# One-core attention and expert-FFN kernel: orders of loads, maxima, probabilities and key projections changed in three attention batches and at the entry of the FFN

## The reference, cut to what matters

```python
def _bi_wkv(r, k, v, w, u, time_emb):     # r = x, k = v = side input
    decay = exp(-exp(w)) * (0.5 + 0.5 * tf)
    nf, df = scan(ekv, ek)                # forward:  a = a * decay + ekv_t
    nb, db = scan(ekv, ek, reverse=True)
    num = nf + nb - ekv + euk * vf
    den = df + db - ek + euk
    return sigmoid(r) * (num / maximum(den, 1e-08)) * (0.8 + 0.2 * tf)

def _L0_attn_ref(query, ...):
    q, k, v = split(query @ Wqkv.T + bqkv)              # 16 heads of 16
    attn = softmax(einsum('bhqd,bhkd->bhqk', q, k) * HD ** 0.5)
    return einsum('bhqk,bhkd->bhqd', attn, v) @ Wproj.T + bproj

def _L0_ffn_ref(x, ...):
    # w_dense: the best 6 of 64 experts, from the best 4 of 8 groups
    h = relu2(einsum('th,eih->tei', x, w1)) * w_dense[:, :, None]
    return einsum('tei,ehi->th', h, w2) + relu2(x @ shared_up.T) @ shared_down.T

x = x + attn(wkv(x, side, ...))
x = x + ffn(wkv2(x, side, ...))
```

## Time and profile before

| | us |
|---|---|
| median of 3 executions | 382.6 (382.35 to 384.66) |
| the profiled execution | 386.37 |
| its span, first to last instruction | 384.3 |
| around the span | 2.07 |
| busy: PE, DVE | 315.8, 319.8 |
| busy: ACT, POOL | 201.6, 129.1 |

### The profile page before, as it was taken

One profiled execution on the slowest core, in us unless ns is written; L12 is line 12 of the kernel. 1 busy time (PEld: TensorE's weight loads), 2 busy tenths in 40 slices (PEclk: granted clock), 3 DMA queues, 4 the chain that ended last, 5 costly groups with the idle time before them and its releaser, 6 DMA issues.

```text
span 384.3 us, 6121 instructions
## 1 busy us (share of the span) xinstructions
PE 315.8 (82%) x1626; PEld 248.8 (65%) x1626; DVE 319.8 (83%) x616; ACT 201.6 (52%) x381; POOL 129.1 (34%) x117
## 2 busy tenths in 40 slices
PE   0082288879678998877898999999999999999994
PEld 0062165658476876744676867788887888888882
DVE  6989999996699977759677999878888888888883
ACT  4113135553624475385447556566666666666651
POOL 2528435424331011032123334343333334343431
PEclk9996577896969999899899999999999999999999
DMA  5949908603550573125433555655556556665631
GB/s 188 160 80 124 191 7 106 112 8 63 96 61 1 103 99 66 69 65 169 140 111 114 168 163 172 191 183 195 196 180 197 185 193 186 195 185 184 194 132 55
DMA packets 36280, 50.79 MB, mean 132 GB/s; under 512 B 5474, under 2 KB 18082, under 8 KB 36258
## 3 DMA queue, kind: packets, MB, share of 16 engines
q1 hardware_dynamic: 36258, 50.52, 51.9%
HBM read 39.03 MB, written 1.33 MB: 105 GB/s over the span
## 4 chain that ended last, share of the span: by engine, by line
PE 52%; DVE 23%; issue 9%; ACT 5%; POOL 5%; DMA 3%; SPq 1%; DVEq 0%; ACTq 0%; POOLq 0%
PE ps L1357 7%; PE ps L1348 7%; PE ps L1346 7%; PE ps L1358 7%; PE ps L1347 7%; PE ps L1359 7%; DVE scan L778 5%; DVE mx L831 5%; PE ps L1184 3%; PE ps L1268 2%; DVE qk_lo L1106 2%; PE ps L1215 2%; ACT prob L520 1%; DVE q_st L986 1%; PE ps L1196 1%
## 5 line engine op out<-in xcount | busy, mean ns | idle before, releaser
L453 POOL TENSOR_TENSOR scan<-scan 128x512 f32<-128x512 f32 x68 | 73.0, 1074 | 130.6 <-ACT scan L583 130.6
L1106 DVE TENSOR_TENSOR qk_lo<-scan,qk_hi 128x512 fp32r<-128x512 f32 x68 | 70.2, 1032 | 26.9 <-ACT qk_hi L590 26.8
L583 ACT ACTIVATE scan<-ps 128x512 f32<-128x512 f32 x68 | 40.8, 600 | 48.3 <-PE ps L1348 48.2
L1357 PE MATMUL ps<-qk_hi,k_st 128*128 128x512 f32 x136 | 55.0, 404 | 3.4 <-DVE qk_lo L1106 3.4
L576 ACT ACTIVATE k_st<-clip 128x512 fp32r<-128x512 f32 x68 | 42.9, 632 | 27.1 <-PE ps L1359 25.4
L1346 PE MATMUL ps<-hid_hi,k_st 128*128 128x512 f32 x136 | 54.3, 399 | 0.8 <-DVE q_st L986 0.8
L1348 PE MATMUL ps<-hid_hi,q_st 128*128 128x512 f32 x136 | 54.2, 399 | 0.0
L1347 PE MATMUL ps<-hid_lo,k_st 128*128 128x512 f32 x136 | 53.9, 396 | 0.0
L1196 PE MATMUL ps<-k_st,q_st 96*128 96x256 f32 x128 | 31.6, 351 | 26.8 <-DVE mx L831 18.7
L1358 PE MATMUL ps<-qk_lo,k_st 128*128 128x512 f32 x136 | 53.4, 393 | 0.0
L1359 PE MATMUL ps<-qk_hi,q_st 128*128 128x512 f32 x136 | 53.3, 392 | 0.0
(11 more groups left out here) (122 smaller groups left out, 487.7 us busy)
## 6 DMA issues: line engine op xcount, KB each, us to landing
clip<-in_tiles SPq DMA_DIRECT2D x68, 256.0 KB, 3.0
ex<-gates SPq DMA_DIRECT2D x136, 128.0 KB, 2.9
q_st<-qk_hi SPq DMA_DIRECT2D x16, 128.0 KB, 3.8
q_st<-qk_lo SPq DMA_DIRECT2D x16, 128.0 KB, 4.7
k_st<-qk_hi SPq DMA_DIRECT2D x16, 128.0 KB, 5.1
k_st<-qk_lo SPq DMA_DIRECT2D x16, 128.0 KB, 5.2
f_sb<-in_fT SPq DMA_DIRECT2D x4, 256.0 KB, 8.8
x_sb<-in_xT SPq DMA_DIRECT2D x4, 256.0 KB, 8.9
```

Source lines behind the costliest of these rows:

```text
L453: g.tensor_tensor(sq[:, k], relu[:, k], relu[:, k], ALU.mult).then_inc(sq_ready, 1)
L1106: TT(act_lo[:, k], act[:, k], act_hi[:, k].bitcast(F32), ALU.subtract).then_inc(act_lo_ready, 1)
L1357: mm(acc, w_hi, act_hi[:, k], start=first, stop=False, skip_group_check=True)
```

## The change

No operation is added or removed. On five queues the order differs; the list `jobs` follows PE's order.

* SP, entry of the FFN: the weights of units 4 and 5 are loaded before the second store of gates, and not behind it.
* PE, batches 1 and 2: the next keys are projected in two pieces, ahead of `values(b - 1, 2)` and of `values(b - 1, 3)`, as batch 0 did already; before, in one piece behind `turn_out`. The gate product goes one head later. In batch 3 `turn_max` stands ahead of `project_out`. With the new list of jobs k waits for q, ot1 for k, oc for ot0 and proj for ot1 (batch 3: m1 for ot1, proj for oc).
* ACT: the high keys are taken right behind `evacuate_o(b - 1, 3)` (batches 0 to 2); some probabilities change places with `round_hidden`, `evacuate_w` and `gate_exp`; in batch 3 the second maxima are negated two heads earlier; the last probability of all goes ahead of `round_act(2)`.
* DVE: `split_qk` of the keys goes ahead of `normalise`; `num_den(b + 2, 0, 0)` goes from the end of a batch behind the second maximum of the next; `hidden2` goes one head later; the router starts one step later; batch 3's residual goes behind `low_max`.

```diff
@@ jobs @@
             jobs += [("m", b, 0)]
+            jobs += [("k", b + 1)] if nxt else []
             jobs += [("ot", b - 1, 0), ("ot", b - 1, 1)] if last else []
-            jobs += [("k", b + 1)] if nxt else []
-            jobs += [("oc", b - 1), ("proj", b - 1)] if last else []
+            jobs += [("oc", b - 1)] if last else []
+            jobs += [("proj", b - 1)] if last and nxt else []
             jobs += [("m", b, 1)]
+            jobs += [] if nxt else [("proj", b - 1)]
@@ SP @@
             store_gates(0)
+            for n in range(RING, RING + 2):
+                sp.wait_ge(t_lo_ready, n - RING + 1)
+                load_raw(n, n % RING)
             store_gates(1)
             sp.wait_ge(st_gates, 32)
             for n in range(SHARED, RING):
                 load_spread(0, n, n)
-            for n in range(RING, HEAD + RING):
+            for n in range(RING, RING + 2):
+                sp.wait_ge(act_ready, n - RING + 1)
+                load_spread(0, n, n % RING)
+            for n in range(RING + 2, HEAD + RING):
                 load_unit(n, 0, n, n % RING)
@@ ACT @@
                     evacuate_v(b)
+                    probabilities(b - 1, HB + 3, HB + 4)
                 if b > 1:
                     round_hidden(b - 2)
-                if b > 0:
-                    probabilities(b - 1, HB + 3, HB + 4)
                 if b > 2:
                     evacuate_w(b - 3)
+                if b > 0:
+                    probabilities(b - 1, HB + 4, HB + 5)
                 if b > 1:
                     gate_exp(b - 2)
-                if b > 0:
-                    probabilities(b - 1, HB + 4, HB + 5)
...
                     evacuate_o(b - 1, 3)
-                if b == 0:
-                    evacuate_qk(1, 1)
-                probabilities(b, 0, 1)
-                if b > 0 and b + 1 < B:
+                if b + 1 < B:
                     evacuate_qk(b + 1, 1)
-                probabilities(b, 1, 2)
+                probabilities(b, 0, 2)
                 if b > 0:
                     evacuate_o_ch(b - 1)
-                probabilities(b, 2, 6)
-                negate_max(b, 1)
-                probabilities(b, 6, 8)
+                if b + 1 < B:
+                    probabilities(b, 2, 6)
+                    negate_max(b, 1)
+                    probabilities(b, 6, 8)
+                else:
+                    probabilities(b, 2, 4)
+                    negate_max(b, 1)
+                    probabilities(b, 4, 8)
...
                 rectify(n, n % 2)
+                if n == 3:
+                    probabilities(B - 1, HB + 7, H)
...
-            probabilities(B - 1, HB + 7, H)
             evacuate_o(B - 1, 3)
@@ DVE @@
                         maximum(b, h)
-                    if h == 1 and b > 1:
+                    if h == 1 and b > 0 and nxt:
+                        num_den(b + 1, 0, 0)
+                    if h == 2 and b > 1:
                         hidden2(b - 2)
-                    if h >= 5:
+                    if h >= 6:
                         next(route_last, None)
...
+                if nxt:
+                    split_qk(b + 1, 1)
                 if b > 0:
                     normalise(b - 1, 0, QT)
...
-                if nxt:
-                    split_qk(b + 1, 1)
                 maximum(b, HB + 6)
...
-                if b > 0:
+                if b > 0 and nxt:
                     residual(b - 1)
...
                 low_max(b, 1)
                 if b + 1 == B:
+                    residual(b - 1)
                     for n in range(2):
                         split_lo(n, n)
...
-                if nxt2:
-                    num_den(b + 2, 0, 0)
@@ PE @@
-                    if b > 1 and h == 3:
+                    if b > 1 and h == 4:
                         gate(b - 2)
...
-                if b == 0:
-                    project(1, "k", 0, 1)
+                if b + 1 < B:
+                    project(b + 1, "k", 0, 1)
                 if b > 0:
                     values(b - 1, 2)
                 scores(b, HB + 2)
                 scores(b, HB + 3)
-                if b == 0:
-                    project(1, "k", 1, KC)
+                if b + 1 < B:
+                    project(b + 1, "k", 1, KC)
                 if b > 0:
                     values(b - 1, 3)
...
-                if b > 0 and b + 1 < B:
-                    project(b + 1, "k")
                 shifted_scores(b, 1)
...
+                if b + 1 == B:
+                    turn_max(b, 1)
                 if b > 0:
                     project_out(b - 1)
...
-                turn_max(b, 1)
+                if b + 1 < B:
+                    turn_max(b, 1)
```

## The result

The changed kernel took 386.8 us (median of 11 executions) against 382.6 for the kernel before on the same chip: ratio 1.0119, with a 95% interval of 1.0094 to 1.0144. It is 1.2% slower, 4.2 us by the medians, where 0.65% faster was forecast. The time lies outside the range, 2.2 us above its upper end.

A forecast was written before the change was run, and what follows sets the result against it. PE bounds from 200 us on; in attention the bound alternates between DVE and PE. Terms 2.7 - 0.8 - 1.3 + 0.3 - 0.6 + 2.2 gain 2.5 us: 382.6 becomes 380.1, range 376.0 to 384.6.

The forecast's parts named there:

- (a): Batch boundaries, numerator behind the second maximum: batch 2 starts 3.7 us earlier, DVE gives back 1.0; gain 2.7, bounds 2.3 to 3.0.
- (b): Batch 0, key split ahead of maximum 12: PE's wait for a maximum grows by 0.85; loss 0.8 us, bounds 0 to 1.1.
- (c, d): Batches 2 and 1, keys in two pieces ahead of the turned outputs: together 1.0 us lost.
- (e): Batch 3, turned maxima ahead of the projection: PE waits 0.85 us for the last maximum; loss 0.6, bounds 0 to 0.9.
- (f): FFN's entry, earlier weight loads and last probability: ACT and PE wait less; gain 2.2 us, bounds 1.0 to 2.4.
- small moves: Gate, router step, hidden2, probabilities against round_hidden: exchange half a microsecond of work with a gap beside it; no effect.
- The same 2.5 us from it give 380.1: Last step: the summed gain of 2.5 us, taken from the trace, is subtracted from the median of 382.6.
- (d): Batch 1's keys: loss of 0.4 us if the low clock stretch stays, gain of 1.5 if it goes; taken as +0.3.
- (c): Batch 2's keys: new wait 1.2 us in the turned outputs, further 0.5, less 0.4 filled; loss 1.3, bounds 0.8 to 2.0.
- Rival A: Low clock leaves batch 1, batch 3's projection and FFN units 2 and 3: 4.0 us on top, 376.1; chance 0.28.
- Rival B: Low clock comes to batch 2's turned outputs, and the same in batch 1: 2.5 us slower, 385.1; chance 0.12.
- Rival C: Gains at the FFN's entry and the batch boundary are eaten by DVE meeting POOL and router steps: 382.4; chance 0.15.

The follow-up runs named there:

- e4: Kernel before with only both numerators (batches 1 and 2) moved behind the second maximum of the next batch: 382.1 us, 0.9979.
- e5: Kernel before with only batch 0's split of batch 1's keys moved ahead of maximum 12: 383.9 us, 1.0025.
- e6: Kernel before with only the keys of batches 1 and 2 projected ahead in two pieces, batch 0's split left: 385.7 us, 1.0075.
- e15: Kernel before with only batch 3's turned maxima ahead of the projection: 383.6 us, 1.003.
- e13: Changed kernel with batch 3's old order put back (turned maxima, residual and negation behind the projection): 386.1 us, 1.0098.
- e3: Kernel before with only the FFN's entry changed (weights 4 and 5 loaded earlier, last probability behind rectify(3)): 381.3 us, 0.9959.
- e16: Kernel before with only the small moves (hidden2, router step, gate matmuls, two probabilities): 380.9 us, 0.9957.
- e2: Changed kernel with the keys of batches 1 and 2 and batch 0's split put back as before: 381.2 us, 0.9959.
- e1: Kernel before, unchanged, profiled once more: 382.5 us, 0.9989, trace span 380.2 us.
- e12: Kernel before with the keys of batches 1 and 2 ahead of the turned outputs, in one piece behind the last values: 388.8 us, 1.0148.
- e14: Changed kernel with batch 1's numerator put back to the end of batch 0: 386.9 us, 1.0121.
- e9: Kernel before plus keys of batches 1 and 2 ahead and the numerators behind the second maximum: 386.1 us, 1.0101.

## Why the prediction was wrong, by its steps

| part | forecast, us | measured alone, us |
|---|---|---|
| (a) numerators | -2.7 | -0.8 (e4) |
| (b) batch 0's split | +0.8 | +1.0, not told from 0 (e5) |
| (c, d) keys of batches 2 and 1 | +1.0 | +2.9 (e6) |
| (e) batch 3's order | +0.6 | +1.1 (e15), +0.8 (e13) |
| (f) FFN's entry | -2.2 | -1.6 (e3) |
| small moves | 0 | -1.6 (e16) |
| sum | -2.5 | +1.0 |
| the change as a whole | -2.5 | +4.2 by the medians, +4.6 by the ratio |

The sum of the measured parts is +1.0, and its uncertainty is some 3 us, since each part has an interval of about 1 us to either side.

In short: the keys (c, d) were put at a loss of 1.0 us and cost 2.9, and e2 and e6 together show that they turn a gain into a loss. The numerators (a) were put at a gain of 2.7 and give 0.8. The small moves, put at nothing, gain 1.6, and so hide part of this. The forecast's last step, adding the terms, leaves another 3.6 us that no part alone shows.

**The reference of the sum.** "The same 2.5 us from it give 380.1" treated the trace's terms as those of the median. The page's 386.37 beside 382.6 was the warning: the trace held a stretch at 88 to 92 us at 0.50 that e1 doesn't have, worth 2.8 us. Term (d), "if it goes, it is a gain of 1.5", took credit for its removal. In an execution like e1 there is nothing to remove: that step failed by 2 us, +0.3 gained against 1.66 lost.

**(c) and (d), the keys.** The mechanism was right: the second wait inside the turned outputs, forecast 1.2, is 1.04, and e12 speaks for the wait and against the values' delay as the cost. Undersized were the other two numbers. The pieces were to fill 0.4 us of gaps and fill 0.16 (1.43 added ahead, 1.59 gone behind). The "further 0.5" behind the split is 1.26 (2.14 - 1.04 + 0.16): DVE normalises after the split and its maxima come after that, so PE waits 0.2 for normalised outputs and 0.4 for a maximum; the remaining 0.65 is the growth of PE's busy time, for which the forecast had no term. 2.14 instead of 1.3, just above the upper bound of 2.0.

**(a), the numerators.** The wait fell from 4.69 to 0.84 and the gain at the boundary is 3.84, against 3.7 forecast. The give-back was put at 1.0 and is 2.42 in the changed kernel. DVE's part of it is 0.69, at the forecast's lower bound; in e4 it is 2.05, since there `hidden2` stands right behind the numerator (1.60 and 1.76 us, where e1 has 1.45 for `hidden2` alone). What the term left out is PE: the low stretch of the clock, which had lain beside DVE's longest work, lies behind it once PE's wait of 4.69 us is gone, and there PE is the later engine. The sum counted DVE as the bound of the whole half. The prediction named low stretches moving into batch 2 as a sign against itself; one was there before, and it moved from the part where it is free to the part where it costs. "The same move without the wait: no gain" for batch 1 was a loss of 1.4 us on DVE in e4's trace; e14 could not show that it costs the whole kernel anything.

**(e) and (b)** hold within what can be measured. **(f)** holds in each of its marks; its size was 2.2 and is 1.6 (0.6 to 2.6), as DVE's work for normalised outputs and weights is late next.

**The small moves** were costed at nothing because each "exchanges work of half a microsecond with a gap beside it". They gained 1.6 us (0.5 to 2.9), of which 0.72 is shown to be `hidden2` away from POOL: the step looked at lengths and not at whom the moved instruction meets.

**Where the excess is.** Measured together, parts do worse than their sum. All but keys and split (e2) would be 0.9925 by its parts and is 0.9959: 1.3 us. Keys and split cost 1.60% on top of e2 and 1.00% alone: 2.3 us more, and 1.8 of these appear as soon as the numerators are there (e9). 1.3 and 2.3 are the 3.6 us between the parts' sum, 1.0, and the whole, 4.6. The whole difference is barely above its uncertainty of some 3 us, and the pieces of it are about as large as theirs or smaller, so where it arises stays open.

The granted clock, known for every execution, points to TensorE's clock for part of it. Its mean is 0.938 over the executions of the changed kernel and 0.942 to 0.943 over those of the kernel before that ran beside the experiments. As an estimate (span times twice what the mean lacks to 1.00), that is 48 us at the low level against 43 to 44. The parts alone come to about 4 us less than the kernel before, added up: e3 -4, e16 -2, e4 -1, e5 and e6 about 0, e15 +4. Within a kernel, an execution with 1 us more at the low level is longer by 0.26 us. So some 8 us more at the low level than the parts would give are worth 2 us of the 3.6, again with an uncertainty as large as the figure. Which wait brings them is not settled.

**The rivals.** Rival A (the low clock leaves) did not come: it left 88 us, where e1 doesn't have it either, and stood at 78 to 82 (0.58) and 112 to 120 us (0.57). Rival B's 385.1 is nearest in time, but not in its mechanism: the middle of batch 2 ran at 1.00. (Its sum takes 4 us for batch 2 where its own sentence has 3; with 3 it is 384.1.) What B describes is in two of the nine traces that have the keys ahead, e12 behind a wait of 1.54 us and e14 behind one of 1.04, and in none of the eleven others. So B can happen to the changed kernel, too; how many of its executions it happens in is not known. Rival C had the give-back of (a) and (f) and came to 382.4, no change; it had the keys at 1.3 and 0.4.

## What to carry to other kernels

Before a term is taken from a trace, compare its time with the median: this one stood 1% above it, another execution lacked one of its low stretches, and the one doubtful term with a gain sat there. A step moved into a stretch that its engine bounds costs its whole length there, and that length has to be asked for again with its new neighbours: a VectorE instruction of 0.7 us took 1.45 to 1.76 beside GpSimd. When a wait of TensorE is removed, look where the low stretch behind it goes: here 3.8 us won at a boundary became 1.4, since the low level moved from beside VectorE's longest work to where TensorE was needed. Parts measured alone need not add; measure the sum before it is forecast.

## What was not expected of the hardware

A VectorE SCALAR_TENSOR_TENSOR of 128x512 took 0.73 us alone, 1.45 beside a GpSimd sum and 1.76 when it followed a VectorE numerator that had itself met one; GpSimd's sum, 1.26 otherwise, took 1.72 in that case. The Trainium skill (SBUF — State Buffer, section Who interferes with whom) says that a VectorE instruction with two SBUF inputs and a GpSimd instruction that reads SBUF contend for one port pair, and that one of them is blocked while the other holds it. The traces agree for both engines: the 1.45 us end 0.55 after GpSimd's sum does, and in e4 GpSimd's 1.72 end 1.14 after the numerator does, nearly its usual length. The scans over PSUM that ran beside the same GpSimd sum in e16 kept their length (1.25 for two).

Executions of one program place TensorE's low level differently: at 88 to 92 us the kernel before was granted 0.50 in one trace and 1.00 in the other, with spans of 384.3 and 380.2. And a wait of 1.04 us in the turned outputs was followed by a low stretch (0.66 at 128 to 138 us) in e14 and by none in the changed kernel and e6.
